# One cross-attention and FFN kernel: products, output pieces and value products in another order in the step list

## The chip, the cores and the metric

One core of a Trainium2 chip runs the whole layer. The time is device microseconds (us) of one execution, the median over runs; lower is better.

## The reference

Per batch row (8 of them, 128 tokens, width 512, 32 heads of 128), cut to what matters; everything is float32:

```python
h = rmsnorm(layernorm(x), ln_weight)                     # and hidden = layernorm(x)
h_q = (h @ w_q.T);  h_k = (ctx @ w_k.T);  h_v = (ctx @ w_v.T)
score = einsum('bqhd,bkhd->bhqk', h_q, h_k) + position_bias   # no scaling
score = where(mask, score, -inf);  p = where(mask, softmax(score), 0)
x = x + layernorm(x) + (p @ h_v) @ w_out.T
r = softmax(layernorm(x) @ gate_w.T)                     # 8 ways
x = x + (layernorm(x) * (r @ in_scale)) @ sign(weight).T * (r @ out_scale) + bias
```

## The kernel before

`schedule()` makes one list of steps. Every engine walks that same list and takes from it the steps it has a part in, so the place of a step sets its place in each engine's queue at once; semaphores do the rest. There is no other scheduler.

**Products.** Each float32 product is made of three TensorE passes (high by high, high by low, low by high), 128x512 each. The projections of a pair of heads go by a Strassen-like scheme: seven partial products `("P", n, i)` for a group n, each of six matmuls, in two PSUM banks. Products 1, 2, 7 and 4 go to the first bank of the pair (`proj0` from the groups after the first query pairs on), products 6, 5 and 3 to the second (`proj1`). Product 1 starts its bank anew, 2 adds to it, 7 starts it anew, 4 adds to it; 6 starts the second bank, 5 and 3 add to it. After each product its bank is read: 1 and 2 by ScalarE (L930, L934), 6 by VectorE at L1113, 5 at L1117, 7 at L1122, 3 at L1126 and 4 at L1131. A product waits until the reading of the one before it in its bank is done (`take`), as product 1 of a group does for L1131 of the group before. It also waits for its weights' low part, which GpSimd makes at L850 from what ScalarE rounds at L954 (steps `("WX", m, part)`).

**Attention units.** The main loop of `schedule()` runs p from 0 to 13. A pass makes four attention units (j = 4p to 4p + 3: two heads by two halves of the batch), the seven products of one query group, and the eight output pieces `("OUT", p - 1, b)` of the pair of heads before (six matmuls each). A unit j is: scores on TensorE (L1535), bias and mask added on VectorE (`SC`, L1270), row maximum (L1273), exponentials on ScalarE (L1008), normalising on VectorE (`N`: L1278, L1279, L1288), a turn of 32x32 blocks on VectorE (L1293), a way through DRAM that finishes the transpose, and the product with the values on TensorE (`PV`, L1561), two units later; then ScalarE rounds the result (`OH`, L1026) and VectorE makes the low part (`OL`, L1300). An output piece waits for `OL` and, in its PSUM bank (`out0` and `out1` in turn), for the addition (`ADD`, L1310 in the first pair, L1315 in the second, L1318 after them) of the piece two before it. GpSimd adds bias and mask (L862) and sums weights (L838 to L843).

**`aside(j, early, middle, late)`** writes one unit's stretch: `PV` of unit j - 2, scores and exponentials of unit j + 1, the early steps, the load of the turned probabilities, `N` and the turn of unit j + 1, then the middle and the late steps. Four calls make a pass. `outs(o, ...)` lists output pieces of the pair of heads before, `prod[i]` is product i with its reading, and `product(n - 1, 4)` the last product of the group before. The pass p = 0 is written out by hand, p = 1 has calls of its own, p = 2 to 13 share the rest, and p = 13 (`final`) has its own last call, since the last units (56 to 63) follow it in another manner.

## Time and profile before

| | |
|---|---|
| median of 3 runs | 805.37 us (805.34 to 806.15) |
| the profiled execution | 805.34 us, its span 803.5 us |
| granted TensorE clock | 1.000 of full speed over the span |
| TensorE busy | 796.5 us |
| VectorE, ScalarE, GpSimd busy | 637.7, 358.7, 306.6 us |

The span runs from the first to the last instruction; the other 1.84 us lie around it. An engine's busy time can be compared with the span directly. TensorE's records of successive matmuls overlap, since they are pipelined, so its step from start to start is what a matmul costs; 128x512 passes follow each other every 0.23 us.

### The profile page before, as it was taken

To read this page: it belongs to the slowest core of one execution; us is meant where nothing else is said; L and a number is where in the kernel's file an instruction comes from. 1 tells how busy PE (TensorE), PEld (TensorE's weight loads), DVE (VectorE), ACT (ScalarE), POOL (GpSimd) and SP (SyncE) were. 2 spreads that over 40 slices of the span, in tenths; PEclk is the share of its full clock that TensorE was granted. 3 is DMA by queue.
4 is the path that set the end of the run, shared out by engine and by line. 5 is a ranking of instruction groups with operands and counts; after the bars stand their busy time and mean duration, and the time that the engine had idled before them with its cause. 6 is when DMAs were issued, how large, how long until landed. Compare 5 with 4: busy or idle time off the path is not lost.

```text
span 803.5 us, 12698 instructions
## 1 busy us (share of the span) xinstructions
PE 796.5 (99%) x4090; PEld 673.5 (84%) x4090; DVE 637.7 (79%) x1066; ACT 358.7 (45%) x949; POOL 306.6 (38%) x279
## 2 busy tenths in 40 slices
PE   9999999999999999999999999999999999999998
PEld 7888888888888888887888888888888888888886
DVE  6877877886893696888888888888888887877675
ACT  6633432432341353644444444444454445446683
POOL 2113021020120033637445654644565464544136
PEclk9999999999999999999999999999999999999999
DMA  9455674584466558616755666575566557563002
GB/s 302 143 185 183 225 252 136 178 273 162 141 190 207 195 183 275 223 49 205 235 173 169 214 198 204 155 240 177 174 198 210 193 158 239 157 198 138 1 1 106
DMA packets 103217, 145.54 MB, mean 181 GB/s; under 512 B 9944, under 2 KB 74584, under 8 KB 97648
## 3 DMA queue, kind: packets, MB, share of 16 engines
q1 hardware_dynamic: 102720, 144.33, 55.3%
q8 instruction: 34, 0.56, 0.3%
q10 hardware_dynamic: 432, 0.39, 0.2%
q14 instruction: 31, 0.25, 0.1%
HBM read 93.31 MB, written 51.38 MB: 180 GB/s over the span
## 4 chain that ended last, share of the span: by engine, by line
PE 96%; DVE 2%; ACT 1%; issue 1%; DVEq 0%; ACTq 0%
PE out L1441 11%; PE out L1443 11%; PE out L1442 11%; PE proj L1441 10%; PE proj L1443 10%; PE proj L1442 10%; PE o L1561 7%; PE s L1535 7%; PE s L1443 4%; PE s L1441 4%; PE s L1442 4%; PE proj L1637 1%; PE proj L1638 1%; PE t L1589 1%; PE t L1545 1%
## 5 line engine op out<-in xcount | busy, mean ns | idle before, releaser
L1008 ACT ACTIVATE probs<-probs,neg_max 128x128 f32<-128x128 f32 x256 | 99.7, 391 | 124.5 <-DVE neg_max L1273 124.5
L838 POOL TENSOR_TENSOR w_stage<-w_stage 128x256 f32<-128x256 f32 x30 | 24.0, 800 | 264.7 <-DMA w_stage<-in_wk 238.6
L850 POOL TENSOR_TENSOR w_lo<-w_stage,w_hi 128x512 fp32r<-128x512 f32 (+1 forms) x52 | 64.2, 1245 | 133.8 <-ACT w_hi L954 133.8
L1441 PE MATMUL out<-wo_hi,o_hi 128*128 128x512 f32 x224 | 91.5, 409 | 0.0
L1443 PE MATMUL out<-wo_lo,o_hi 128*128 128x512 f32 x224 | 87.9, 392 | 0.0
L1441 PE MATMUL proj<-x_hi,w_hi 128*128 128x512 f32 x210 | 85.8, 409 | 1.8 <-DVE ring L1117 1.8
L1442 PE MATMUL out<-wo_hi,o_lo 128*128 128x512 f32 x224 | 87.4, 390 | 0.0
L862 POOL TENSOR_TENSOR bias_mask<-bias_raw,mask_neg 128x512 f32<-128x512 f32 x64 | 81.2, 1269 | 14.0 <-DVE probs L1270 13.8
L1443 PE MATMUL proj<-x_lo,w_hi 128*128 128x512 f32 x210 | 82.4, 392 | 0.0
L1442 PE MATMUL proj<-x_hi,w_lo 128*128 128x512 f32 x210 | 81.9, 390 | 0.0
L1318 DVE TENSOR_TENSOR acc<-out,acc 128x512 f32<-128x512 f32 x100 | 66.5, 675 | 8.2 <-PE out L1443 8.2
L954 ACT ACTIVATE w_hi<-w_stage 128x512 fp32r<-128x512 f32 (+1 forms) x113 | 61.7, 565 | 17.9 <-POOL w_stage L840 4.4
L1300 DVE TENSOR_TENSOR o_lo<-o,o_hi 128x512 fp32r<-128x512 f32 x60 | 41.2, 686 | 23.8 <-ACT o_hi L1026 23.8
L1026 ACT ACTIVATE o_hi<-o 128x512 fp32r<-128x512 f32 x60 | 35.4, 590 | 41.3 <-PE o L1561 41.2
L1441 PEld LDWEIGHTS out<-wo_hi,o_hi 128*128 128x128 f32 x224 | 42.2, 188 | 11.1 <-issue 3.7
L1138 DVE TENSOR_TENSOR w_lo<-w_stage,w_hi 128x512 fp32r<-128x512 f32 (+1 forms) x61 | 44.8, 735 | 7.3 <-ACT w_hi L954 6.6
L1443 PEld LDWEIGHTS out<-wo_lo,o_hi 128*128 128x128 f32 x224 | 42.0, 188 | 9.3
L1441 PEld LDWEIGHTS proj<-x_hi,w_hi 128*128 128x128 f32 x210 | 39.5, 188 | 11.2 <-DVE ring L1117 4.5
L1442 PEld LDWEIGHTS out<-wo_hi,o_lo 128*128 128x128 f32 x224 | 42.3, 189 | 7.4
L871 POOL TENSOR_TENSOR wo_lo<-wo_raw,wo_hi 128x1024 fp32r<-128x1024 f32 x14 | 34.0, 2428 | 37.4 <-ACT wo_hi L1034 37.4
L1008 ACT ACTIVATION_READ_ACCUMULATOR probs<-probs,neg_max 128x1 f32 x256 | 47.9, 187 | 0.0
L1443 PEld LDWEIGHTS proj<-x_lo,w_hi 128*128 128x128 f32 x210 | 39.4, 188 | 8.7
(360 smaller groups left out, 2080.1 us busy)
## 6 DMA issues: line engine op xcount, KB each, us to landing
k_spill<-ring SPq DMA_DIRECT2D x64, 256.0 KB, 3.5
v_spill<-ring SPq DMA_DIRECT2D x64, 256.0 KB, 2.5
p_turned<-probs SPq DMA_DIRECT2D x208, 64.0 KB, 1.8
probs_t<-p_turned SPq DMA_DIRECT2D x52, 256.0 KB, 4.0
big_stage<-in_wv SPq DMA_DIRECT2D x8, 1024.0 KB, 8.3
w_stage<-in_wq SPq DMA_DIRECT2D x32, 256.0 KB, 3.2
k_first<-k_spill SPq DMA_DIRECT2D x8, 1024.0 KB, 6.2
v_first<-v_spill SPq DMA_DIRECT2D x8, 1024.0 KB, 5.4
```

The costliest lines, as they stand in the source:

```text
L850: pool.tensor_tensor(lo, staged(m, part), hi.bitcast(F32), ALU.subtract).then_inc(g_wlo, 1)
L862: pool.tensor_tensor(bias_mask[:, j % 2], bias_raw[:, i % 2][:, None, :].to_broadcast([P, HALF, P]), mask_neg[:, halves[half], :], ALU.add ...
L954: act.activation(hi, staged(m, part), ACT.Copy).then_inc(a_whi, 1)
L1008: last = act.activation(probs[:, j % 2, b, :], probs[:, j % 2, b, :], ACT.Exp, bias=neg_max[:, col:col + 1], accum_out=row_sum[:, col:col ...
L1138: dve.tensor_tensor(lo, staged(m, part), hi.bitcast(F32), ALU.subtract).then_inc(v_wlo, 1)
L1300: dve.tensor_tensor(lo[:, h % 2], o_bank[:], hi[:, h % 2].bitcast(F32), ALU.subtract).then_inc(v_olo, 1)
L1318: dve.tensor_tensor(acc[:, b, :], bank_tensor[:], acc[:, b, :], ALU.add).then_inc(v_acc, 1)
L1441: pe.matmul(to[:], left_hi, right_hi, start=first and n == 0, stop=False, skip_group_check=True)
L1442: pe.matmul(to[:], left_lo, right_hi, start=False, stop=False, skip_group_check=True)
L1443: last = pe.matmul(to[:], left_hi, right_lo, start=False, stop=n == len(pairs) - 1, skip_group_check=True)
L1535: last = pe.matmul(to[:, b * P:(b + 1) * P], queries[:, b * P:(b + 1) * P], keys, start=True, stop=True)
L1561: last = pe.matmul(to[:, b * P:(b + 1) * P], v_tiles[p % 2][:, half * HALF + b, i * P:(i + 1) * P], moving, start=True, stop=True)
```

## The change

Only the order in the list changes; no instruction is added or taken away. In p = 0 the third output piece of the pair is taken in at the end. In p = 1 the pieces and products move among the four stretches: product 6 comes before the normalising of its stretch, product 2 to the end of it, product 5 a stretch earlier. In p = 2 to 13 the second output piece of the first stretch goes behind product 1. In p = 13 the value product of unit 54 goes behind product 3.

```diff
-                      *outs(0, 0), *normal(4), ("KL", 2), *sums, *outs(0, 1)]
+                      *outs(0, 0), *normal(4), ("KL", 2), *sums, *outs(0, 1, 2)]
...
         if p == 1:
-            steps += aside(j, outs(o, 2, 3) + prod[1], [("WX", m, 1)], [])
-            steps += aside(j + 1, load + outs(o, 4, 5), [*prod[6], ("VV", p + 1), ("WX", m, 2), ("WX", m, 3)], [])
-            steps += aside(j + 2, outs(o, 6) + prod[2], [*sums[:1], *outs(o, 7)], [("WO", p)])
-            steps += aside(j + 3, prod[5] + prod[7], [("WOL", p + 1), *prod[3], ("KL", p + 2), *sums[1:]], [])
+            steps += aside(j, outs(o, 3) + prod[1], [*outs(o, 4), ("WX", m, 1)], [])
+            steps += aside(j + 1, load + outs(o, 5) + prod[6], [("VV", p + 1), ("WX", m, 2), ("WX", m, 3)], prod[2])
+            steps += aside(j + 2, outs(o, 6), [*prod[5], *sums[:1], *outs(o, 7)], [("WO", p)])
+            steps += aside(j + 3, prod[7], [*prod[3], ("WOL", p + 1), ("KL", p + 2), *sums[1:]], [])
             continue
-        steps += aside(j, product(n - 1, 4) + outs(o, 0), [*outs(o, 1), *prod[1], ("WX", m, 1)], [])
+        steps += aside(j, product(n - 1, 4) + outs(o, 0), [*prod[1], ("WX", m, 1)], outs(o, 1))
...
         if final:
-            steps += aside(j + 3, prod[5] + prod[7], [("WOL", p + 1), ("PV", j + 2), *prod[3], *prod[4], ("KL", p + 2), ("WO", p + 1)],
+            steps += aside(j + 3, prod[5] + prod[7], [("WOL", p + 1), *prod[3], ("PV", j + 2), *prod[4], ("KL", p + 2), ("WO", p + 1)],
                            [*outs(p, 0, 1), ("PV", j + 3), ("VV", p + 2)])
```

TensorE in the first stretch of p = 2, from the last matmul of output piece (1, 0) in `out1` on. The rows give line, operation, result and inputs, and what a row waits for. Before, piece (1, 1) in `out0` follows and then product 1 in `proj0`:

```order
L1443 MATMUL out1<-wo_lo,o_hi 128x512
L1441 MATMUL out0<-wo_hi,o_hi 128x512 [waits v_acc,v_olo,g_wo_lo]
L1442 MATMUL out0<-wo_hi,o_lo 128x512
L1443 MATMUL out0<-wo_lo,o_hi 128x512
L1441 MATMUL out0<-wo_hi,o_hi 128x512
L1442 MATMUL out0<-wo_hi,o_lo 128x512
L1443 MATMUL out0<-wo_lo,o_hi 128x512
L1441 MATMUL proj0<-x_hi,w_hi 128x512 [waits g_wlo,v_read]
```

The same place with the change:

```order
L1443 MATMUL out1<-wo_lo,o_hi 128x512
L1441 MATMUL proj0<-x_hi,w_hi 128x512 [waits g_wlo,v_read]
L1442 MATMUL proj0<-x_hi,w_lo 128x512
L1443 MATMUL proj0<-x_lo,w_hi 128x512
L1441 MATMUL proj0<-x_hi,w_hi 128x512
L1442 MATMUL proj0<-x_hi,w_lo 128x512
L1443 MATMUL proj0<-x_lo,w_hi 128x512
L1441 MATMUL out0<-wo_hi,o_hi 128x512 [waits v_acc,v_olo,g_wo_lo]
```

Product 1 and its wait on VectorE's reading (`v_read`, L1131) stand six matmuls earlier. VectorE's own order is the same there.

VectorE in p = 1, from the addition of output piece (0, 6) on. Before:

```order
L1310 SCALAR_TENSOR_TENSOR acc<-acc,res_scale,out 128x512
L1278 RECIPROCAL inv_sum<-row_sum 128x4
L1279 TENSOR_TENSOR inv_sum<-inv_sum,row_valid 128x4
L1288 TENSOR_TENSOR t<-probs,inv_sum 128x512
L1293 STREAM_TRANSPOSE probs<-t 128x4x4x32
L1310 SCALAR_TENSOR_TENSOR acc<-acc,res_scale,out 128x512
L1300 TENSOR_TENSOR o_lo<-o,o_hi 128x512
L1270 TENSOR_TENSOR probs<-s,bias_mask 128x512
L1273 TENSOR_REDUCE neg_max<-probs 128x4
L1117 TENSOR_TENSOR ring<-proj,ring 128x512
L1122 TENSOR_TENSOR ring<-proj,ring 128x512
```

With the change:

```order
L1310 SCALAR_TENSOR_TENSOR acc<-acc,res_scale,out 128x512
L1278 RECIPROCAL inv_sum<-row_sum 128x4
L1279 TENSOR_TENSOR inv_sum<-inv_sum,row_valid 128x4
L1288 TENSOR_TENSOR t<-probs,inv_sum 128x512
L1293 STREAM_TRANSPOSE probs<-t 128x4x4x32
L1117 TENSOR_TENSOR ring<-proj,ring 128x512
L1310 SCALAR_TENSOR_TENSOR acc<-acc,res_scale,out 128x512
L1300 TENSOR_TENSOR o_lo<-o,o_hi 128x512
L1270 TENSOR_TENSOR probs<-s,bias_mask 128x512
L1273 TENSOR_REDUCE neg_max<-probs 128x4
L1122 TENSOR_TENSOR ring<-proj,ring 128x512
```

The reading of product 5 (L1117) stands ahead of the next unit's scores (L1270) instead of behind its maximum.

VectorE at the end of p = 13, as a difference:

```order
 L1279 TENSOR_TENSOR inv_sum<-inv_sum,row_valid 128x4
 L1288 TENSOR_TENSOR probs<-probs,inv_sum 128x512
-L1300 TENSOR_TENSOR o_lo<-o,o_hi 128x512
-L1126 TENSOR_TENSOR ring<-proj,ring 128x512
+L1126 TENSOR_TENSOR ring<-proj,ring 128x512
+L1300 TENSOR_TENSOR o_lo<-o,o_hi 128x512
 L1131 TENSOR_TENSOR ring<-proj,ring 128x512
 L1318 TENSOR_TENSOR acc<-out,acc 128x512 x2
```

The low part of unit 54's result (L1300) stands behind the reading of product 3.

## Rows read from the trace of the kernel before

**Rows 1.** The page's first part: busy us (share of the span) and instructions.

```profile
PE 796.5 (99%) x4090; PEld 673.5 (84%) x4090; DVE 637.7 (79%) x1066; ACT 358.7 (45%) x949; POOL 306.6 (38%) x279
```

**Rows 2.** Waits of TensorE, 330 to 700 us: waiting and releaser, us, times, longest.

```profile
PE proj L1441 <- DVE ring L1117: 1.8, 1, 1.8
```

**Rows 3.** Timeline of VectorE in p = 1: start, length, line, operation, idle before.

```profile
356.65 0.70 DVE L1310 SCALAR_TENSOR_TENSOR acc<-acc,res_scale,out 128x512 f32<-128x512 f32 x1
...
357.87 0.68 DVE L1270 TENSOR_TENSOR probs<-s,bias_mask 128x512 f32<-128x512 f32 x1
...
362.77 0.65 DVE L1270 TENSOR_TENSOR probs<-s,bias_mask 128x512 f32<-128x512 f32 x1
...
367.65 0.65 DVE L1113 TENSOR_TENSOR ring<-proj,ring 128x512 f32<-128x512 f32 x1
368.23 0.68 DVE L1300 TENSOR_TENSOR o_lo<-o,o_hi 128x512 fp32r<-128x512 f32 x1
368.82 0.68 DVE L1270 TENSOR_TENSOR probs<-s,bias_mask 128x512 f32<-128x512 f32 x1
...
372.75 1.19 DVE L1288 TENSOR_TENSOR t<-probs,inv_sum 128x512 f32<-128x512 f32 x1
...
375.84 0.68 DVE L1270 TENSOR_TENSOR probs<-s,bias_mask 128x512 f32<-128x512 f32 x1
...
377.15 0.68 DVE L1117 TENSOR_TENSOR ring<-proj,ring 128x512 f32<-128x512 f32 x1
```

**Rows 4.** Timeline of ScalarE in p = 1: two high parts of weights.

```profile
365.74 1.13 ACT L954 ACTIVATE w_hi<-w_stage 128x512 fp32r<-128x512 f32 x2
```

**Rows 5.** Timeline of TensorE around its only stall in the passes.

```profile
375.71 0.39 PE L1443 MATMUL proj<-x_lo,w_hi 128*128 128x512 f32 x1
377.88 0.50 PE L1441 MATMUL proj<-x_hi,w_hi 128*128 128x512 f32 x1 [1.79 <-DVE ring L1117]
378.22 0.39 PE L1442 MATMUL proj<-x_hi,w_lo 128*128 128x512 f32 x1
378.45 0.39 PE L1443 MATMUL proj<-x_lo,w_hi 128*128 128x512 f32 x1
```

**Rows 6.** Timeline of TensorE's weight loads at the same stall.

```profile
377.88 0.19 PEld L1441 LDWEIGHTS proj<-x_hi,w_hi 128*128 128x128 f32 x1 [2.21 <-DVE ring L1117]
```

**Rows 7.** Timeline of TensorE: output pieces' first matmuls, p = 2 and p = 13.

```profile
382.61 0.47 PE L1441 MATMUL out<-wo_hi,o_hi 128*128 128x512 f32 x1
...
384.07 0.40 PE L1441 MATMUL out<-wo_hi,o_hi 128*128 128x512 f32 x1
...
691.85 0.39 PE L1441 MATMUL out<-wo_hi,o_hi 128*128 128x512 f32 x1
```

**Rows 8.** Timeline of VectorE: p = 2, end of p = 2, first stretch of p = 13.

```profile
381.83 0.67 DVE L1300 TENSOR_TENSOR o_lo<-o,o_hi 128x512 fp32r<-128x512 f32 x1
...
383.74 0.68 DVE L1131 TENSOR_TENSOR ring<-proj,ring 128x512 f32<-128x512 f32 x1
...
407.37 1.22 DVE L1288 TENSOR_TENSOR t<-probs,inv_sum 128x512 f32<-128x512 f32 x1
...
691.54 0.68 DVE L1131 TENSOR_TENSOR ring<-proj,ring 128x512 f32<-128x512 f32 x1
```

**Rows 9.** Timeline of GpSimd at the end of p = 2.

```profile
407.31 0.72 POOL L850 TENSOR_TENSOR w_lo<-w_stage,w_hi 128x256 fp32r<-128x256 f32 x1 [0.99 <-ACT w_hi L954]
```

**Rows 10.** Line 1131, 370 to 740 us: ns min/median/max, first and last start.

```profile
L1131 DVE TENSOR_TENSOR ring<-proj,ring x13: 680/681/691, 383.7 to 717.5; 128x512 f32<-128x512 f32 x13
```

**Rows 11.** Timeline at the end of p = 13, TensorE: value product, first output piece.

```profile
713.70 1.05 PE L1561 MATMUL o<-probs_t,v_second 128*128 128x128 f32 x8
...
717.34 0.39 PE L1441 MATMUL out<-wo_hi,o_hi 128*128 128x512 f32 x1
```

**Rows 12.** The same place, ScalarE: high part of unit 54's result.

```profile
714.79 0.60 ACT L1026 ACTIVATE o_hi<-o 128x512 fp32r<-128x512 f32 x1
```

**Rows 13.** The same place, VectorE: low part of unit 54's result.

```profile
715.71 0.68 DVE L1300 TENSOR_TENSOR o_lo<-o,o_hi 128x512 fp32r<-128x512 f32 x1
```

## The prediction

> **What bounds the kernel now.** I read the busy times first: TensorE is busy for 796.5 of 803.5 us [rows 1], so some 7 us are all that any change of order can give, and most of that lies at the start and the end of the span. Then its waits in the passes of the main loop: there is one, 1.8 us, on the reading of product 5 (L1117) in p = 1 [rows 2]. Everywhere else TensorE goes through. So a change of order can win here once, and it can lose at every place where it puts a matmul ahead of what it needs. What is late at such a place is read from the timeline of VectorE beside that of TensorE.
>
> Two prices are needed throughout. **What a stall costs:** in p = 1 the matmul before it started at 375.71, so the next was due at 375.94 and the one after at 376.17, at 0.23 us a matmul (378.22 to 378.45 [rows 5]). L1117 ended at 377.15 + 0.68 = 377.83 [rows 3]; the matmul started at 377.88 and the second at 378.22 [rows 5]. So the second came 0.39 after the release, and the loss is 378.22 - 376.17 = 2.05 us, more than the 1.79 shown. As a rule: loss = release + 0.39 - (due + 0.23) = release + 0.16 - due. **What a product costs TensorE:** six matmuls, 1.37 us.
>
> **Part 1, p = 2 to 13: output piece 1 goes behind product 1.** VectorE's order doesn't change there, nor ScalarE's; only TensorE reaches product 1 six matmuls earlier. Product 1 starts bank `proj0` anew and so waits for L1131, which reads product 4 of the group before out of it. In p = 2 output piece 1 started at 384.07 [rows 7]; with the change product 1 is due then. L1131 ran from 383.74 to 384.42 [rows 8]: 0.35 too late, a loss of 0.51. In p = 13 it is 691.54 + 0.68 = 692.22 against 691.85 [rows 7, 8]: 0.37 late, a loss of 0.53. L1131 runs 13 times, the last in the final stretch [rows 10], so 12 passes have this pair, and the distance is between 0.35 and 0.37 in all of them. Nothing gives it back: L1131 can't come earlier, since VectorE goes without a break from the normalising of the stretch before (407.37 in p = 2 [rows 8]) to it, and the start of that is set by TensorE's product 7 in each pass anew, so all of it is shifted along with TensorE. What is behind the waiting matmul on TensorE, piece 1 and then the next unit's value product and scores, comes 0.5 later; VectorE's addition of piece 1 and all else wait for that or had slack. The earlier reading of product 1 by ScalarE frees ScalarE for L1026 a little sooner (some 0.1 us), which TensorE has no use for. Sum: 12 x 0.52 = **+6.2 us**. From below: if the restart costs only its 0.05 to the first matmul, 12 x 0.41 = 4.9.
>
> TensorE: Matmul & The Clock Gate in the Trainium skill (section Step-by-step: what each phase is for) says that weight loads are pulled ahead of running matmuls; by that rule the new stall would hide its load and cost 0.41 each, 4.9 in all. The trace doesn't show it for a matmul that waits: the load starts with the matmul, at 377.88, having waited for the same release [rows 6]. So 0.52 stands.
>
> **Part 2, p = 0 and 1: the stall at 376 goes, but what is late next?** VectorE and ScalarE run one chain here, unit by unit: scores plus bias (L1270), maximum, exponentials, normalising, turn, then whatever stands before the next L1270. The four L1270 start at 357.87, 362.77, 368.82 and 375.84 [rows 3], steps of 4.90, 6.05 and 7.02; and L1300 of unit 6, on which the first output piece of p = 2 waits, starts 5.99 after the last, at 381.83, ends at 382.50, and that piece starts at 382.61 [rows 7, 8]. So TensorE's start of p = 2 is set by this chain as much as the stall was. Operations between the maximum and the normalising lie beside the exponentials and are free; those between the turn and the next L1270 lengthen the chain. The change moves them so:
> - addition of piece 2 goes ahead of the first L1270, of piece 4 ahead of the second: +0.70 each [rows 3]. L1270s at 358.57 and 362.77 + 0.70 + 0.70 = 364.17.
> - the reading of product 6 (L1113) goes beside the exponentials: the step from 367.65 to 368.23, -0.58 [rows 3]. But L1300 of unit 4 behind it then waits for ScalarE: the two high parts start 2.97 after L1270 (365.74 - 362.77) [rows 3, 4], so at 367.14, and take 1.13; then come product 2's reading and L1026, 0.60 each [rows 12]; a length runs some 0.1 into the next one's start. That is 369.27 for L1300, and L1270 follows 0.59 later (368.23 to 368.82) at 369.86: 1.04 later than before.
> - product 5's reading (L1117) goes from beside the exponentials into the chain: +0.60. L1288 at 372.75 took 1.19 because GpSimd was at its weight sums; how the two meet now is the open term. Without any meeting the stretch loses up to 0.9, with the same one nothing; I take 0.3 less than before.
> So the last L1270 comes at 369.86 + 7.02 + 0.60 - 0.3 = 377.2, and L1300 of unit 6 ends at 377.2 + 5.99 + 0.67 = 383.9. The first output piece of p = 2 starts 0.11 after that, at 384.0, instead of 382.61. TensorE doesn't stall at product 3 any more (L1117 ends at about 376), reaches that piece at 380.6 and waits there for some 3.3 us. The stall is moved, and it grows: **+1.4 us** (0.75 to 1.7 by the meeting of L1288 with GpSimd). A lesser point: product 6 now wants its weights at 364.05 and GpSimd has them at about 364.0; up to 0.2 is lost there, but inside the 3.3.
>
> SBUF — State Buffer in the Trainium skill (section Who interferes with whom) has an exclusive lock for VectorE's operations with two SBUF inputs against GpSimd; the rows agree, L1288 took 1.22 while L850 held 0.72 of it [rows 8, 9].
>
> **Part 3, the end of p = 13: value product of unit 54 behind product 3.** The value product started at 713.70 [rows 11] and L1026 1.09 later, at 714.79 [rows 12]; L1300 waited for nothing but VectorE at 715.71 [rows 13]. Behind product 3 the value product starts at 715.07, L1026 at 716.16, L1300 at 716.79, and ends at 717.47. The first output piece, which needs it, is due at 717.34 as before [rows 11]: loss 717.47 + 0.16 - 717.34 = **+0.3 us**.
>
> **The sum** against the profiled execution, 805.34 us (0.03 under the median, so the same): 805.34 + 6.2 + 1.4 + 0.3 = **813.2 us**. Its own range: 0.75 + 4.9 + 0 below, 811.0; above 1.7 + 6.4 + 0.5 and a little for terms unseen, 814.5. SyncE's and GpSimd's orders don't change, and the turned probabilities have two units' time to come back, so no DMA comes into it.
>
> **The rivals.**
> - The stall at 376 falls away and nothing takes its place: 805.34 - 2.05 = 803.3, faster. It needs L1131 at least 0.5 earlier against TensorE in 12 passes, and L1300 of unit 6 at least 2 earlier. For it: the stall is real. Against it: both operations stand where they stood on VectorE.
> - The chain in p = 1 isn't as stiff as I read it and the stall does vanish, while the wait on L1131 costs its 6.2 and the end 0.3: 805.34 - 2.05 + 6.5 = 809.8. For it: p = 1 is a sum of many terms. Against it: two operations more in the chain.
> - The wait on L1131 resolves itself: L1288 ran 1.22 instead of 0.70 since GpSimd began 0.06 before it [rows 8, 9]. If the new order parts the two, L1131 comes 0.52 earlier and product 1 loses nothing: 805.34 + 1.7 = 807.0. Against it: both follow ScalarE's exponentials in that stretch, whose order is the same.
> - The earlier reading of product 1 moves GpSimd's L850 in the first stretch and the later piece 1 moves VectorE's additions; if L1288 of the second stretch now meets GpSimd (before they missed each other by about 0.1 us) and the 0.5 reaches TensorE, 12 x 0.52 more: 819.4. Against it: VectorE waits for ScalarE again before the next L1300, which takes that up.
> - The moves have no effect that can be told from none, the gain in p = 1 paying for shorter waits elsewhere.
>
> **How the numbers follow.** The forecast has 0.68, the second rival 0.10, the third 0.07, the fourth 0.07, the first 0.06, no effect 0.02. Predicted is 813.2. To hold 8 in 10 the range takes in the second rival and the forecast's own: 809.5 to 815.0. A measurement of this kernel tells about 0.2% (1.6 us) from no change; the third rival is at the edge of that and counts as slower. Faster 0.06, the same 0.03, slower 0.91.
>
> **What would show it.** After the change the waits of TensorE must have product 1 (L1441 in `proj`) behind L1131, 12 times, 0.2 to 0.4 us each by the profile's count; the first output piece of p = 2 must wait about 3 us, with L1300 as releaser or just ahead; the wait on L1117 must be gone or under 0.6. The pass lasted (691.85 - 384.07) / 11 = 27.98 us before [rows 7] and must last 28.5. If TensorE shows no wait on L1131, part 1 is wrong and with it the sign's size; if the first piece of p = 2 starts before 382.6, part 2 is wrong.

## The result, and the profile after

| | before | after |
|---|---|---|
| median | 805.76 us (805.34 to 806.17) | 814.55 us (813.24 to 814.86) |
| the profiled execution | 805.34 us, span 803.5 | 813.57 us, span 811.8 |
| granted TensorE clock over the span | 1.000 | 1.000 |
| TensorE busy | 796.5 us | 800.1 us |

The change makes the kernel slower by 8.8 us: after over before is 1.0106, 95% interval 1.0089 to 1.0124. Forecast were 813.2 us and a range of 809.5 to 815.0. The profiled execution took 8.2 us more.

The page of the changed kernel, busy us of each engine; it answers to [rows 1]:

```profile
PE 800.1 (99%) x4090; PEld 672.0 (83%) x4090; DVE 637.4 (79%) x1066; ACT 360.3 (44%) x949; POOL 306.8 (38%) x279
```

The 8 us don't stand out there: a matmul that waited has a longer record (0.50 instead of 0.39), and short gaps go unseen. The waits of the changed kernel's TensorE in the same stretch as [rows 2], 330 to 705 us (us, times, longest), show them at once:

```profile
PE proj L1441 <- DVE ring L1131: 3.1, 12, 0.3
PE out L1441 <- issue: 2.4, 1, 2.4
PE o L1561 <- DMA probs_t<-p_turned: 0.4, 1, 0.4
```

The wait on L1117 is gone. In its place stand the twelve waits of product 1, one long wait of an output piece, and a short one of a value product that wasn't foreseen. First the repeated one: VectorE's reading of product 4 at the start of p = 2 of the changed kernel, then TensorE from the last matmul of output piece 0 on, and the first output piece of p = 13:

```profile
385.08 0.68 DVE L1131 TENSOR_TENSOR ring<-proj,ring 128x512 f32<-128x512 f32 x1
```

```profile
385.18 0.39 PE L1443 MATMUL out<-wo_lo,o_hi 128*128 128x512 f32 x1
385.82 0.50 PE L1441 MATMUL proj<-x_hi,w_hi 128*128 128x512 f32 x1 [0.25 <-DVE ring L1131]
386.15 0.39 PE L1442 MATMUL proj<-x_hi,w_lo 128*128 128x512 f32 x1
...
697.74 0.47 PE L1441 MATMUL out<-wo_hi,o_hi 128*128 128x512 f32 x1
```

Product 1 was due at 385.18 + 0.23 = 385.41 and its second matmul at 385.64; that came at 386.15. The loss is 0.51, of which the profile counts 0.25 as idle. L1131 ended at 385.76, so release + 0.16 - due gives 385.76 + 0.16 - 385.41 = 0.51 as well. The first output piece of p = 2 starts at 383.95 (below), that of p = 13 at 697.74: a pass lasts (697.74 - 383.95) / 11 = 28.53 us, and was 27.98 [rows 7].

Now p = 1. VectorE of the changed kernel, to be laid beside [rows 3] and [rows 8]:

```profile
356.10 0.72 DVE L1293 STREAM_TRANSPOSE probs<-t 128x512 f32<-128x512 f32 x1
...
358.63 0.68 DVE L1270 TENSOR_TENSOR probs<-s,bias_mask 128x512 f32<-128x512 f32 x1
...
364.15 0.68 DVE L1270 TENSOR_TENSOR probs<-s,bias_mask 128x512 f32<-128x512 f32 x1
...
369.88 0.68 DVE L1270 TENSOR_TENSOR probs<-s,bias_mask 128x512 f32<-128x512 f32 x1
...
373.21 0.22 DVE L1279 TENSOR_TENSOR inv_sum<-inv_sum,row_valid 128x4 f32<-128x4 f32 x1
373.47 1.19 DVE L1288 TENSOR_TENSOR t<-probs,inv_sum 128x512 f32<-128x512 f32 x1
...
375.33 0.65 DVE L1117 TENSOR_TENSOR ring<-proj,ring 128x512 f32<-128x512 f32 x1
...
377.15 0.68 DVE L1270 TENSOR_TENSOR probs<-s,bias_mask 128x512 f32<-128x512 f32 x1
...
383.17 0.67 DVE L1300 TENSOR_TENSOR o_lo<-o,o_hi 128x512 fp32r<-128x512 f32 x1
```

Two more rows of VectorE from the kernel before, to compare with 356.10 and 373.21:

```profile
356.01 0.72 DVE L1293 STREAM_TRANSPOSE probs<-t 128x512 f32<-128x512 f32 x1
...
372.15 0.56 DVE L1279 TENSOR_TENSOR inv_sum<-inv_sum,row_valid 128x4 f32<-128x4 f32 x1
```

And TensorE of the changed kernel, where the stall of before was ([rows 5]) and where the new one is:

```profile
376.21 0.40 PE L1441 MATMUL proj<-x_hi,w_hi 128*128 128x512 f32 x1
...
378.10 1.16 PE L1561 MATMUL o<-probs_t,v_second 128*128 128x128 f32 x8 [0.36 <-DMA probs_t<-p_turned]
...
381.15 0.40 PE L1443 MATMUL proj<-x_lo,w_hi 128*128 128x512 f32 x1
383.95 0.47 PE L1441 MATMUL out<-wo_hi,o_hi 128*128 128x512 f32 x1 [2.40 <-issue]
```

Product 3 goes through at 376.21 without a wait. The output piece was due at 381.38 and waits until 383.95. The profile names "issue", which is no releaser; L1300 of unit 6 had ended at 383.84, 0.11 before, and is the one: of what else this piece waits for, VectorE's last L1310 had ended at 376.64 and GpSimd's last L871 at 377.63. So the stall moved from product 3 to the first output piece of p = 2, and grew.

### The profile page after: what moved, and what is told of

Its sections match the earlier page's. It is cut to its first block, busy times and chain, and to the rows that moved or that the text cites. A ratio compares the mean times of both kernels' runs of the same rounds, so it can differ in the third digit from the quotient of the medians.

```text
span 811.8 us, 12698 instructions
## 1 busy us (share of the span) xinstructions
PE 800.1 (99%) x4090; PEld 672.0 (83%) x4090; DVE 637.4 (79%) x1066; ACT 360.3 (44%) x949; POOL 306.8 (38%) x279
## 4 chain that ended last, share of the span: by engine, by line
PE 81%; DVE 10%; issue 4%; ACT 4%; DMA 0%; ACTq 0%; DVEq 0%
PE out L1441 10%; PE out L1443 10%; PE out L1442 10%; PE proj L1441 8%; PE proj L1443 8%; PE proj L1442 8%; PE o L1561 4%; PE s L1535 4%; PE s L1442 4%; PE s L1443 4%; PE s L1441 4%; ACT probs L1008 2%; DVE probs L1270 2%; DVE t L1288 2%; DVE neg_max L1273 1%
## 5 line engine op out<-in xcount | busy, mean ns | idle before, releaser
L850 POOL TENSOR_TENSOR w_lo<-w_stage,w_hi 128x512 fp32r<-128x512 f32 (+1 forms) x52 | 63.9, 1238 | 140.5 <-ACT w_hi L954 140.5
L1300 DVE TENSOR_TENSOR o_lo<-o,o_hi 128x512 fp32r<-128x512 f32 x60 | 41.2, 687 | 28.0 <-ACT o_hi L1026 27.8
L871 POOL TENSOR_TENSOR wo_lo<-wo_raw,wo_hi 128x1024 fp32r<-128x1024 f32 x14 | 33.6, 2401 | 38.7 <-ACT wo_hi L1034 38.7
```

The costliest lines, as they stand in the source:

```text
L850: pool.tensor_tensor(lo, staged(m, part), hi.bitcast(F32), ALU.subtract).then_inc(g_wlo, 1)
L871: pool.tensor_tensor(lo, wo_raw[:], hi.bitcast(F32), ALU.subtract).then_inc(g_wo_lo, 1)
L1300: dve.tensor_tensor(lo[:, h % 2], o_bank[:], hi[:, h % 2].bitcast(F32), ALU.subtract).then_inc(v_olo, 1)
```

## The experiments

Each kernel is the kernel before with the edit shown. Times of one batch are compared with runs of the kernel before on the same chip: 805.73 us for the first four, 805.78 for the next four, 805.65 for the last four. In edits, `("ONLY", ...)` writes a part of a step alone, where the plain step would bring its companion with it (an output piece its addition, `PV` its `OH` and `OL`).

### The three parts, one by one

**Part 1 alone**, p = 2 to 13:

```diff
-        steps += aside(j, product(n - 1, 4) + outs(o, 0), [*outs(o, 1), *prod[1], ("WX", m, 1)], [])
+        steps += aside(j, product(n - 1, 4) + outs(o, 0), [*prod[1], ("WX", m, 1)], outs(o, 1))
```

> Only the move in p = 2 to 13: output piece 1 behind product 1. Theory (a matmul put ahead of the reading it needs): product 1 waits for L1131 in each of 12 passes, 0.2 to 0.4 us each as the profile counts idle time, 0.52 us each in real loss with the restart; 805.7 + 6.2 = 811.9 us (810.6 if a stall costs only what the profile shows as idle and 0.05 for the restart). The stall on L1117 in p = 1 stays, 1.8. Rival (the moves of p = 0 and 1 carry the loss): within 1 us of before.

Measured: 812.02 us (811.62 to 812.38), ratio 1.0078, interval 1.0066 to 1.0090, so +6.3. Waits of its TensorE:

```profile
PE proj L1441 <- DVE ring L1131: 3.1, 12, 0.3
PE proj L1441 <- DVE ring L1117: 1.6, 1, 1.6
```

Twelve waits, 3.1 us by the profile, cost 6.3 us of time. The rule with 0.52 a stall holds, the counted idle of 0.26 doesn't. The old stall on L1117 is still there, so nothing is given back elsewhere.

**Part 2 alone**, p = 0 and 1:

```diff
-                      *outs(0, 0), *normal(4), ("KL", 2), *sums, *outs(0, 1)]
+                      *outs(0, 0), *normal(4), ("KL", 2), *sums, *outs(0, 1, 2)]
...
-            steps += aside(j, outs(o, 2, 3) + prod[1], [("WX", m, 1)], [])
-            steps += aside(j + 1, load + outs(o, 4, 5), [*prod[6], ("VV", p + 1), ("WX", m, 2), ("WX", m, 3)], [])
-            steps += aside(j + 2, outs(o, 6) + prod[2], [*sums[:1], *outs(o, 7)], [("WO", p)])
-            steps += aside(j + 3, prod[5] + prod[7], [("WOL", p + 1), *prod[3], ("KL", p + 2), *sums[1:]], [])
+            steps += aside(j, outs(o, 3) + prod[1], [*outs(o, 4), ("WX", m, 1)], [])
+            steps += aside(j + 1, load + outs(o, 5) + prod[6], [("VV", p + 1), ("WX", m, 2), ("WX", m, 3)], prod[2])
+            steps += aside(j + 2, outs(o, 6), [*prod[5], *sums[:1], *outs(o, 7)], [("WO", p)])
+            steps += aside(j + 3, prod[7], [*prod[3], ("WOL", p + 1), ("KL", p + 2), *sums[1:]], [])
```

> Only the moves in p = 0 and 1. Theory (the chain of VectorE and ScalarE from unit to unit is what ends there, two operations longer): the wait on L1117 is gone, the first output piece of p = 2 waits some 2.4 us for L1300, as in the changed kernel; 805.7 + 1.4 = 807.1 us. Rival (the stall on L1117 was the bound): 2 us faster than before, 803.7.

Measured: 807.68 us (806.75 to 809.52), ratio 1.0025, interval 1.0015 to 1.0035. The eight executions fall into two groups: 806.75 to 807.03 with a granted clock of 1.000 over the span, and 808.34 to 809.52 with 0.995 to 0.997. The first group is +1.2 and agrees with the chain as worked out. The second has something more, and the profiled execution (809.52) is one of it. Its windows of 2 us (after the window: busy us of the engines; the third number from the end is PEclk, the granted clock):

```profile
380.00:382.00 2.00, 1.14 (x5) 0.57 (x4) 1.43 (x3) 1.25 (x5) 1.15 (x2) 1.00 0.65 166
382.00:384.00 2.00, 0.00 (x0) 0.00 (x0) 1.97 (x5) 0.00 (x0) 1.13 (x1) 0.87 0.11 29
384.00:386.00 2.00, 1.84 (x5) 1.50 (x5) 1.94 (x4) 0.59 (x3) 0.00 (x0) 0.50 0.47 111
...
390.00:392.00 2.00, 2.00 (x13) 1.73 (x12) 0.41 (x1) 0.58 (x2) 0.00 (x0) 0.92 0.93 333
```

Its TensorE there:

```profile
377.80 1.05 PE L1561 MATMUL o<-probs_t,v_second 128*128 128x128 f32 x8
...
384.16 0.77 PE L1441 MATMUL out<-wo_hi,o_hi 128*128 128x512 f32 x1 [3.02 <-issue]
384.72 0.63 PE L1442 MATMUL out<-wo_hi,o_lo 128*128 128x512 f32 x1
...
390.26 0.43 PE L1443 MATMUL proj<-x_lo,w_hi 128*128 128x512 f32 x1
```

During the wait of 3.02 us the clock goes from 1.00 to 0.50, that is from 2.4 to 1.2 GHz, and stays there for some 6 us of work. From 384.72 to 390.26 there are 13 steps of 0.43 instead of 0.23, which is 13 x 0.20 = 2.6 us, and the step before them took 0.56 instead of 0.31: 2.9 us in all, where 809.52 lies 2.6 over the group at 806.9. The prediction has no term for it.

**Part 3 alone**, the value product of unit 54:

```diff
-            steps += aside(j + 3, prod[5] + prod[7], [("WOL", p + 1), ("PV", j + 2), *prod[3], *prod[4], ("KL", p + 2), ("WO", p + 1)],
+            steps += aside(j + 3, prod[5] + prod[7], [("WOL", p + 1), *prod[3], ("PV", j + 2), *prod[4], ("KL", p + 2), ("WO", p + 1)],
```

> Only the move in p = 13: the value product of unit 54 behind product 3. Theory: the output piece behind product 4 waits for L1300, a loss of 0.3 us, 806.0 us, which a time can hardly tell from before; the profile can, by the start of that piece against the value product before it. Rival: no loss at all.

Measured: 806.16 us (805.13 to 809.33), ratio 1.0007, interval 0.9998 to 1.0015. By time alone it can't be told from nothing. The timeline of this kernel shows the loss, first TensorE, then VectorE's L1300:

```profile
717.86 0.39 PE L1443 MATMUL proj<-x_lo,w_hi 128*128 128x512 f32 x1
718.34 0.47 PE L1441 MATMUL out<-wo_hi,o_hi 128*128 128x512 f32 x1
718.65 0.39 PE L1442 MATMUL out<-wo_hi,o_lo 128*128 128x512 f32 x1
```

```profile
717.55 0.69 DVE L1300 TENSOR_TENSOR o_lo<-o,o_hi 128x512 fp32r<-128x512 f32 x1 [0.44 <-ACT o_hi L1026]
```

The second matmul was due at 717.86 + 0.46 = 718.32 and came at 718.65: 0.33, where 0.3 was worked out; in the changed kernel the same three matmuls start at 725.08, 725.54 and 725.85, which is 0.31. The profile counts no wait of a matmul here: by the records TensorE stands still from 718.25 to 718.34 only.

### Is it the reading, or the order of TensorE?

Product 1 waits for L1131 because VectorE does the next unit's scores and maximum first. This kernel has TensorE's order of part 1, and VectorE reads product 4 (L1131, the step `C21`) ahead of the scores (L1270, `SC`):

```diff
-        steps += aside(j, product(n - 1, 4) + outs(o, 0), [*outs(o, 1), *prod[1], ("WX", m, 1)], [])
+        first = aside(j, product(n - 1, 4) + outs(o, 0), [*prod[1], ("WX", m, 1)], outs(o, 1))
+        first[first.index(("S", j + 1))] = ("ONLY", ("S", j + 1))
+        first.insert(first.index(("C21", n - 1)) + 1, ("ONLY", ("SC", j + 1)))
+        steps += first
```

> The move in p = 2 to 13 as in the run of that move alone, TensorE's order the same to the matmul, but on VectorE the reading of product 4 (L1131) stands ahead of the next unit's scores (L1270), not behind its maximum. Theory (product 1 waits for L1131 and for nothing else): L1131 ends at about 0.7 after product 4, some 0.6 before product 1 is due; the 12 waits are gone, and the scores, some 0.9 later, are taken up by VectorE's idle time before L1300 in the next three stretches: 805.7 us within 0.5. Rival (TensorE's own order, its bank changes, costs the time): 811.9 as with the move alone. Third: the later scores reach product 3 or the next pass's first output piece and cost part of it, 807 to 810.

Measured: 805.97 us (805.32 to 806.42), ratio 1.0001, interval 0.9993 to 1.0010. The wait on L1131 is gone from the list. VectorE and TensorE of this kernel in p = 3:

```profile
411.51 0.69 DVE L1131 TENSOR_TENSOR ring<-proj,ring 128x512 f32<-128x512 f32 x1 [0.23 <-PE proj L1443]
412.12 0.68 DVE L1270 TENSOR_TENSOR probs<-s,bias_mask 128x512 f32<-128x512 f32 x1
```

```profile
411.38 0.47 PE L1441 MATMUL out<-wo_hi,o_hi 128*128 128x512 f32 x1
...
412.84 0.39 PE L1441 MATMUL proj<-x_hi,w_hi 128*128 128x512 f32 x1
```

Now L1131 waits for the product and not the product for L1131; product 1 starts 1.46 after the piece, six matmuls as they run elsewhere, with nothing lost. All of part 1's 6.2 us hang on where that one reading of 0.68 us stands; what TensorE's order costs by itself is too small to be told from nothing, 0.8 us at most by the interval.

### Small losses that the profile doesn't count

If a stall costs release + 0.16 - due, it also costs something where the release comes a little before the matmul is due. In p = 3 of the kernel before, for one, L1300 ends at 410.51 and the first output piece is due at 410.56, 0.05 later. This kernel moves the reading of product 3 (L1126, `C12`), which stands ahead of L1300, behind the next unit's maximum:

```diff
-            steps += aside(j + 3, prod[5] + prod[7], [("WOL", p + 1), *prod[3], ("KL", p + 2), *sums[1:]], [])
+            steps += aside(j + 3, prod[5] + prod[7], [("WOL", p + 1), prod[3][0], ("KL", p + 2), *sums[1:]], [])
...
-        steps += aside(j, product(n - 1, 4) + outs(o, 0), [*outs(o, 1), *prod[1], ("WX", m, 1)], [])
+        steps += aside(j, [("C12", n - 1)] + product(n - 1, 4) + outs(o, 0), [*outs(o, 1), *prod[1], ("WX", m, 1)], [])
...
         else:
-            steps += aside(j + 3, prod[5] + prod[7], [("WOL", p + 1), *prod[3], ("KL", p + 2), *sums[1:]], [])
+            steps += aside(j + 3, prod[5] + prod[7], [("WOL", p + 1), prod[3][0], ("KL", p + 2), *sums[1:]], [])
```

> The kernel before, with one move on VectorE alone: the reading of product 3 (L1126) stands behind the next unit's maximum in p = 2 to 13 instead of ahead of L1300. The first output piece of each pass waits for L1300 now (0.11 from its end to the piece, the weights' load late by 0.29), a loss of 0.13 a pass by the rule release + 0.16 - due. Theory (that rule holds for waits too short to be counted as TensorE's idle time): L1300 0.58 earlier, 12 x 0.13 = 1.5 us faster, 804.2. Rival (only idle time that the profile counts is lost time): no change, 805.7.

Measured: 803.54 us (802.92 to 804.56), ratio 0.9974, interval 0.9963 to 0.9986: 2.2 us faster than the kernel before. The weight loads' waits of the whole span, before and then in this kernel:

```profile
PEld out L1441 <- issue: 4.5, 15, 0.3
```

```profile
PEld out L1441 <- issue: 0.8, 3, 0.3
```

Twelve short waits of 0.3 are gone, and they were waits of weight loads, not of matmuls. Product 4 to product 1 of p = 3 took 409.09 to 413.45 = 4.36 us before and 409.00 to 413.19 = 4.19 here; 12 x 0.17 = 2.0 of the 2.2. Of the 0.17, 0.13 lies at the piece itself, as expected; the cause of the rest wasn't looked for. The rule for a late release holds here too: 410.51 + 0.16 - 410.56 = 0.11.

### How stiff is the chain in p = 1?

**L1113 and the addition of piece (0, 7) beside the exponentials**, which should shorten the chain by two operations:

```diff
-            steps += aside(j + 1, load + outs(o, 4, 5), [*prod[6], ("VV", p + 1), ("WX", m, 2), ("WX", m, 3)], [])
-            steps += aside(j + 2, outs(o, 6) + prod[2], [*sums[:1], *outs(o, 7)], [("WO", p)])
-            steps += aside(j + 3, prod[5] + prod[7], [("WOL", p + 1), *prod[3], ("KL", p + 2), *sums[1:]], [])
+            steps += aside(j + 1, load + outs(o, 4, 5) + prod[6], [("VV", p + 1), ("WX", m, 2), ("WX", m, 3)], [])
+            steps += aside(j + 2, outs(o, 6) + prod[2], [*sums[:1], ("ONLY", ("OUT", o, 7))], [("WO", p)])
+            steps += aside(j + 3, prod[5] + [("ONLY", ("ADD", o, 7))] + prod[7], [("WOL", p + 1), *prod[3], ("KL", p + 2), *sums[1:]], [])
```

> The kernel before, TensorE's order the same, VectorE's changed in p = 1 alone: the reading of product 6 (L1113) and the addition of output piece 7 stand beside the exponentials instead of ahead of the scores. Theory (chain): 1.21 out of the chain, some 0.38 back because three operations don't fit beside one set of exponentials; the reading of product 5 (L1117) is 0.9 to 1.0 earlier, the stall of 1.8 shrinks to 0.9, and 804.8 us. Rival (what GpSimd's lock does to L1288 decides, and eats it): 805.7.

Measured: 806.36 us (805.64 to 808.83), ratio 1.0015, interval 1.0004 to 1.0026. A miss: no gain. The seven executions at a clock of 1.000 have a median of 805.95, so most of the 0.6 is the clock. TensorE waits 2.3 us for L1117, where it waited 1.8 [rows 2]. VectorE, and GpSimd beside it:

```profile
366.80 1.27 DVE L1279 TENSOR_TENSOR inv_sum<-inv_sum,row_valid 128x4 f32<-128x4 f32 x1
368.10 1.75 DVE L1288 TENSOR_TENSOR t<-probs,inv_sum 128x512 f32<-128x512 f32 x1
```

```profile
366.77 2.53 POOL L850 TENSOR_TENSOR w_lo<-w_stage,w_hi 128x512 fp32r<-128x512 f32 x2 [1.97 <-ACT w_hi L954]
```

L1279 takes 0.16 where nothing is beside it; here it began 0.03 after GpSimd's first of two 1.26 us operations and ended with it, and L1288 (0.70 alone) then lost to the second. That is 1.11 + 1.05 = 2.16 us on the chain. In return the next stretch, where the kernel before loses 0.40 + 0.49 = 0.89 by L1279 (0.56) and L1288 (1.19), loses nothing here: they take 0.16 and 0.70. The lock's net cost is 1.27, which eats the 1.2 that was taken out, and from the first to the last L1270 it is 18.53 us where it was 17.97 [rows 3]. SBUF — State Buffer in the Trainium skill (section Who interferes with whom) calls the ports that VectorE and GpSimd share an exclusive lock, and says that the order of issue decides who is blocked; these rows agree, twice in a row.

**Both of the last two edits together**; the last call of p = 1 then reads:

```diff
-            steps += aside(j + 3, prod[5] + prod[7], [("WOL", p + 1), *prod[3], ("KL", p + 2), *sums[1:]], [])
+            steps += aside(j + 3, prod[5] + [("ONLY", ("ADD", o, 7))] + prod[7], [("WOL", p + 1), prod[3][0], ("KL", p + 2), *sums[1:]], [])
```

> Both of the two last moves together. Theory: they add up, 0.9 and 1.5, 803.3 us, with TensorE stalled once in the passes, for 0.9 us. Rival: the one takes from the other, 804 or more.

Measured: 805.69 us (803.36 to 806.77), ratio 0.9994, interval 0.9985 to 1.0003. A miss. L1279 and L1288 took 0.96 and 1.76, the wait at product 3 was 2.0, and seven of eleven executions had a granted clock of 0.997 or 0.998 and took 805.4 to 806.8; the four at 0.999 or above took 803.4 to 804.8. So most of the gain of the moved reading is there at the higher clock, and the stall in p = 1 takes it back where the clock falls.

**Part 2 with the additions of pieces 2 and 4 beside the exponentials**, to see whether the +0.70 each is what part 2 pays:

```diff
-                      *outs(0, 0), *normal(4), ("KL", 2), *sums, *outs(0, 1, 2)]
+                      *outs(0, 0), *normal(4), ("KL", 2), *sums, *outs(0, 1), ("ONLY", ("OUT", 0, 2))]
...
-            steps += aside(j, outs(o, 3) + prod[1], [*outs(o, 4), ("WX", m, 1)], [])
-            steps += aside(j + 1, load + outs(o, 5) + prod[6], [("VV", p + 1), ("WX", m, 2), ("WX", m, 3)], prod[2])
+            steps += aside(j, [("ONLY", ("ADD", o, 2))] + outs(o, 3) + prod[1], [("ONLY", ("OUT", o, 4)), ("WX", m, 1)], [])
+            steps += aside(j + 1, load + [("ONLY", ("ADD", o, 4))] + outs(o, 5) + prod[6], [("VV", p + 1), ("WX", m, 2), ("WX", m, 3)], prod[2])
```

> The moves of p = 0 and 1 as in the run of those alone, TensorE's order the same to the matmul, but VectorE's additions of output pieces 2 and 4 stand behind the next maximum, beside the exponentials, instead of ahead of the next scores. Theory (the end of p = 1 is set by the chain of VectorE and ScalarE, which the move made two operations longer): the chain loses 1.40 less 0.25 for the third operation beside the second exponentials, so L1300 of unit 6 ends 1.1 to 1.4 earlier, the first output piece of p = 2 waits 1.2 us instead of 2.4 to 3.0, the clock stays at its upper level, and the time is that of before within 0.5: 805.8 us. Rival (TensorE's order in p = 1 costs the time): 807 or more, as with the move.

Measured: 808.44 us (808.16 to 809.46), ratio 1.0038, interval 1.0026 to 1.0051. A miss, and for the same reason as the one above: the chain is shorter at its start and not at its end. The two rows of VectorE where the gain goes, and the wait that stays:

```profile
368.75 0.69 DVE L1300 TENSOR_TENSOR o_lo<-o,o_hi 128x512 fp32r<-128x512 f32 x1 [0.43 <-ACT o_hi L1026]
...
372.70 0.62 DVE L1279 TENSOR_TENSOR inv_sum<-inv_sum,row_valid 128x4 f32<-128x4 f32 x1
```

```profile
383.82 0.47 PE L1441 MATMUL out<-wo_hi,o_hi 128*128 128x512 f32 x1 [2.94 <-issue]
```

VectorE comes early and waits for ScalarE (0.43, and 0.26 once before), and then L1279 meets GpSimd's weight sums (0.62, where part 2 alone has 0.21). From the turn ahead of the moved addition to the first output piece of p = 2 it is 383.82 - 356.13 = 27.69 us, and 384.16 - 356.33 = 27.83 in part 2 alone: 0.14 of the expected 1.1 to 1.4. This chain can't be read as a plain sum of its operations' lengths. All five executions had a clock of 0.995 to 0.998, so their 808.44 is to be laid beside the 808.8 of part 2's executions at the lower clock, and not beside 806.9.

**Only the addition of piece (0, 7)** beside the exponentials, L1113 where it was:

```diff
-            steps += aside(j + 2, outs(o, 6) + prod[2], [*sums[:1], *outs(o, 7)], [("WO", p)])
-            steps += aside(j + 3, prod[5] + prod[7], [("WOL", p + 1), *prod[3], ("KL", p + 2), *sums[1:]], [])
+            steps += aside(j + 2, outs(o, 6) + prod[2], [*sums[:1], ("ONLY", ("OUT", o, 7))], [("WO", p)])
+            steps += aside(j + 3, prod[5] + [("ONLY", ("ADD", o, 7))] + prod[7], [("WOL", p + 1), *prod[3], ("KL", p + 2), *sums[1:]], [])
```

> The kernel before with one operation moved: in p = 1 VectorE does the addition of output piece (0, 7) (L1310) behind the reading of product 5 (L1117), beside the exponentials, instead of between the turn and the next L1270. Theory of the stiff chain: the last L1270 of p = 1 comes 0.63 earlier less about 0.1 for GpSimd's lock, at some 375.3 instead of 375.84, L1117 ends at 377.3, the stall of TensorE at product 3 shrinks from 1.8 to about 1.3, and the kernel takes 0.5 to 0.6 us less: 805.2. Rival (the lock, as when L1113 was moved too): with VectorE's L1288 starting in another moment against GpSimd's weight sums, L1279 and L1288 take longer by as much as was won: stall of 1.8 or more, 805.8 or above. Here the L1288 that runs against GpSimd in the stretch before isn't moved, so I hold the first for likelier, 2 to 1.

Measured: 804.91 us (804.42 to 805.85), ratio 0.9987, interval 0.9979 to 0.9996: 0.7 us faster. Its TensorE:

```profile
376.86 0.50 PE L1441 MATMUL proj<-x_hi,w_hi 128*128 128x512 f32 x1 [0.70 <-DVE ring L1117]
```

The profiled execution shows more than the edit takes out: the last L1270 comes 17.03 after the first, against 17.97 [rows 3], 0.63 for the addition and the rest because L1279 took 0.28 in it and 0.56 before. Whether the lock's share changes from one execution of this kernel to the next, which span 1.4 us, isn't shown; the kernel with both gains, below, has the same order up to there, and in its trace L1279 took 0.56 again.

**Part 2 with the reading of product 5 (L1117) back beside the exponentials**, against part 2:

```diff
-            steps += aside(j + 2, outs(o, 6), [*prod[5], *sums[:1], *outs(o, 7)], [("WO", p)])
-            steps += aside(j + 3, prod[7], [*prod[3], ("WOL", p + 1), ("KL", p + 2), *sums[1:]], [])
+            steps += aside(j + 2, outs(o, 6), [prod[5][0], *sums[:1], *outs(o, 7)], [("WO", p)])
+            steps += aside(j + 3, [prod[5][1]] + prod[7], [*prod[3], ("WOL", p + 1), ("KL", p + 2), *sums[1:]], [])
```

> Part 2 of the change alone, with the reading of product 5 (L1117) put back to where it was, beside the exponentials of the next unit. It settles the third item of part 2 of the prediction (L1117 in the chain costs 0.60). Theory: the last L1270 of p = 1 comes 0.6 earlier than with part 2 alone (at some 376.5 instead of 377.1), TensorE stalls at product 3 again, by about 2.4, and the first output piece of p = 2 starts 0.6 earlier than with part 2 alone, at some 383.3, having waited little: 806.9 - 0.6 = 806.3 for executions with the clock at 1.00. Rival: the meeting with GpSimd changes again and the 0.60 isn't had back: 806.9 or more. In either case the stall of 2.4 may bring the clock down to 0.50 for some us in part of the executions, which adds 1.5 to 2.5 to those.

Measured: 806.36 us (805.78 to 807.68), ratio 1.0011, interval 1.0002 to 1.0019. The eight executions at a clock of 1.000 took 805.78 to 806.51, the four at 0.998 took 806.93 to 807.68. The last L1270 and the reading:

```profile
376.85 0.68 DVE L1270 TENSOR_TENSOR probs<-s,bias_mask 128x512 f32<-128x512 f32 x1
...
378.16 0.68 DVE L1117 TENSOR_TENSOR ring<-proj,ring 128x512 f32<-128x512 f32 x1
```

```profile
378.90 0.50 PE L1441 MATMUL proj<-x_hi,w_hi 128*128 128x512 f32 x1 [2.25 <-DVE ring L1117]
...
383.63 0.47 PE L1441 MATMUL out<-wo_hi,o_hi 128*128 128x512 f32 x1
```

From the first L1270 (358.91) to the last it is 17.94, in part 2 alone 358.85 to 377.38 = 18.53: 0.59 for L1117, as worked out, and the executions at a clock of 1.000 are 0.7 us faster than those of part 2 alone (806.2 against 806.9). And in this kernel TensorE stands for 2.25 at product 3 and reaches the first output piece with almost nothing to wait for: one and the same delay shows at either place. That is what "the stall is moved" means.

### A version that beats both

**The reading of product 3 late, and the addition of piece (0, 7) beside the exponentials**, the two edits that gained; both diffs stand above, and the last call of p = 1 is that of the kernel with both of the two edits.

> The kernel before with two edits: the addition of piece (0, 7) beside the exponentials in p = 1, and in p = 2 to 13 the reading of product 3 (L1126) behind the next unit's maximum. The second alone gave 803.54. Theory that the two add: 803.54 - 0.6 = 802.9, and TensorE's one stall at product 3 of p = 1 at about 1.3. Rival: the addition of piece (0, 7) gives nothing, or its later place in front of the reading of product 3 costs what it gives: 803.5.

Measured: 803.27 us (802.66 to 803.51), ratio 0.9966, interval 0.9954 to 0.9978. TensorE waits 1.1 on L1117, more than the 0.7 with the addition alone, for the most part since L1279 took 0.56 and not 0.28. The 0.3 below 803.54 is less than the 0.6 expected and within the spread of both.

**The same, with TensorE's value product of unit 6 ahead of product 3**, to fill the stall:

```diff
-        found = [("PV", j - 2)] if j - 2 in BLOCKED else [("PV", 3)] if j == 4 else []
+        found = [("ONLY", ("OH", 6), ("OL", 6))] if j == 8 else [("PV", j - 2)] if j - 2 in BLOCKED else [("PV", 3)] if j == 4 else []
...
-            steps += aside(j + 3, prod[5] + [("ONLY", ("ADD", o, 7))] + prod[7], [("WOL", p + 1), prod[3][0], ("KL", p + 2), *sums[1:]], [])
+            steps += aside(j + 3, prod[5] + [("ONLY", ("ADD", o, 7))] + prod[7], [("WOL", p + 1), ("ONLY", ("PV", 6)), prod[3][0], ("KL", p + 2), *sums[1:]], [])
```

> The two edits of the run before and a third: in p = 1 TensorE does the value product of unit 6 (L1561, 0.89 us of TensorE) ahead of product 3 instead of behind it, so that it runs while product 3 waits for the reading of product 5 (L1117). VectorE's order is that of the run before. Theory that the stall is only an order of TensorE: the value product's operands are there at about 375.5, it starts at about 376 when TensorE would idle, the stall at product 3 shrinks from 1.3 to about 0.4, and the kernel takes 0.9 us less than without it: 802.0. The idle being short, the granted clock should stay at 1.00 there in all executions. Rival: what ends the stretch is the chain of VectorE up to L1300 of unit 6, before which the first output piece of p = 2 waits; then the gain at product 3 turns into a wait of that piece, and the time stays at 802.9. Second rival: the value product waits for the DMA that brings the turned probabilities, by 0.4 as in the changed kernel; 802.4.

Measured: 802.89 us (802.29 to 803.48), ratio 0.9963, interval 0.9952 to 0.9975: the fastest, 2.8 us under the kernel before, though not to be told from the one above it (803.27). Its only wait in the passes:

```profile
PE o L1561 <- DMA probs_t<-p_turned: 0.9, 1, 0.9
```

The wait on L1117 is gone, and the value product waits in its place, for the turned probabilities to come back. That is the second rival of the expectation, with a wait of 0.9 where it had 0.4; so little of the 1.1 is won, and the time is the 802.9 that the first rival had, but not for its reason: the first output piece of p = 2 doesn't wait here.

## Why the prediction came right

**Part 1, 6.2 us: right, with its mechanism.** Part 1 alone measured +6.3, with twelve waits of product 1 on L1131. The price of a stall was the step that mattered: 4.9 if the load were hidden, 3.1 by the profile's own count, 6.2 by the rule. The weight load is held up with its matmul; the changed kernel's loads show 0.7 for each where its matmuls show 0.3:

```profile
PEld proj L1441 <- DVE ring L1131: 8.2, 12, 0.7
```

The third rival, L1131 coming earlier, would have shown as no wait. The fourth, a second collision, would have made the pass 28.53 + 0.52 = 29.05 us; it lasts 28.53, and L1288 of the second stretch, at 387.29, still takes 0.70. The reading moved by hand took all of it away, which is the other side of the same proof. One reading of the prediction was a little off: of L1288's 1.22 us GpSimd's L850 overlaps 0.66 and not 0.72, as it had begun 0.06 earlier; no sum uses it.

**Part 2, 1.4 us: right in its mechanism, and a little too large in its size at full clock.** The chain was forecast operation by operation:

| | forecast | changed kernel |
|---|---|---|
| L1270, first | 358.57 | 358.63 |
| second | 364.17 | 364.15 |
| third | 369.86 | 369.88 |
| last | 377.2 | 377.15 |
| first output piece of p = 2 | 384.0 | 383.95 |

That the times of the table agree to hundredths is luck in part. In ten of the kernels here, which have the same order up to the first L1270, it starts anywhere from 357.79 to 358.68, so distances are the better test. From the turn (L1293) ahead of it to the first output piece of p = 2 it was 382.61 - 356.01 = 26.60 us; it is 27.85 in the changed kernel and 27.83 with part 2 alone: +1.25 and +1.23, where +1.4 was forecast. The two additions were put at +0.70 each, their length, and cost 0.67 and 0.62, as a length runs into the next one's start. The last term took 0.3 off for a meeting of L1288 with GpSimd, a choice between 0 and 0.9 without a row behind it. Its size came true by another operation: L1288 took 1.19 as before, and L1279 in front of it 0.22 instead of 0.56. It was 0.21 and 0.23 in the two other kernels of this order, so it isn't the luck of one execution; but where the order differs, the lock took between 0.6 and 2.2 us from the first to the last L1270, and the prediction couldn't know which.

The wait at the output piece was put at 3.3 and counted at 2.4 in the changed kernel, and at 3.0 in part 2 alone. The difference is that TensorE reached the piece at 381.38 and not at 380.6, in part for a reason the prediction had ruled out ("no DMA comes into it"): the value product of unit 6 was due at 377.58 and started at 378.10, as its turned probabilities weren't back. In part 2 alone it started at 377.80, without a wait; so the DMA is late in some executions and not in all. Those 0.5 us cost nothing, as they lie ahead of the longer wait. The direction of part 2 is shown (+1.2 at full clock); that it could be had to a tenth isn't.

**Part 3, 0.3 us: 0.31 in the timeline of the changed kernel and 0.33 by itself**, and too small to be measured as a time.

**The sum.** 813.2 was forecast; the profiled execution took 813.57, the median is 814.55. The parts measured one by one, 6.3 + 1.2 (at full clock) + 0.3, on 805.76 give 813.6, so they add up and don't act on each other much. What the sum left out is the clock. Of the five executions of the changed kernel two had 0.998 over the span, and took 814.68 and 814.86; those at 1.000 took 813.24, 813.57 and 814.43. So the clock explains a part of the 1.3 us between forecast and median, and the spread of the rest isn't explained. The stated range held it, with 0.45 us to spare above; the sum's own upper end, 814.5, is just below it.

**The rivals.** That the stall vanishes and nothing takes its place fell with the wait of 2.4 us. The second, a chain that isn't stiff, fell in the changed kernel but is half true: with L1113 moved (two kernels) and with the additions of pieces 2 and 4 moved, ScalarE and the lock took all or nearly all of it back, while the addition of piece (0, 7) alone kept its 0.63 and L1117 put back its 0.59. That nothing can be told from no change fell with the interval, 1.0089 to 1.0124.

## What to carry to other kernels

Before a product is moved earlier on the engine that sets the time, look up when its buffer's last reading ends on the other engine; a reading 0.35 us late costs 0.51 us each time, in every pass, and may be cured by moving that one reading. Look also for waits of weight loads of 0.2 to 0.3 us that repeat once a pass: they don't appear as waits of matmuls, and twelve of them were worth 2.2 us here. (Eleven more, of 0.2 us, stand at product 3 of the kernel before, behind L1117. In p = 2 the step there is 405.94 to 406.24, 0.30 instead of 0.23, so they may be worth 11 x 0.07 = 0.8 us by this estimate; no run tried it.) A chain over several engines isn't a sum of lengths; when one of its operations shares a lock with another engine, every move re-deals who comes first.

## What the runs showed of the hardware

**A wait of 2 to 3 us of TensorE can halve its clock, in one execution and not in the next.** The changed kernel's windows over its wait of 2.4 us, in its profiled execution, against those of part 2 alone above:

```profile
382.00:384.00 2.00, 0.05 (x1) 0.09 (x1) 2.00 (x4) 0.00 (x0) 0.92 (x1) 1.00 0.15 37
384.00:386.00 2.00, 1.75 (x7) 1.15 (x8) 1.97 (x4) 0.80 (x5) 0.00 (x0) 1.00 0.44 105
```

Here the clock stays at 1.00. Over all timed executions the mean granted clock was 0.998 or less in:

| kernel | longest wait in p = 1, us | executions at 0.998 or less |
|---|---|---|
| addition of piece (0, 7) beside | 0.7 | 0 of 12 |
| the two fastest | 0.9 and 1.1 | 0 of 11 |
| part 1 alone; reading 4 first; reading 3 late | 1.6 to 1.8 | 0 of 23 |
| before, in the three batches; part 3 alone | 1.8 and 1.7 | 7 of 84 |
| L1113 and addition beside, with and without reading 3 late | 2.0 and 2.3 | 11 of 22 |
| part 2, reading of product 5 beside | 2.3 | 4 of 12 |
| the changed kernel | 2.4 | 2 of 5 |
| part 2 alone | 3.0 | 4 of 8 |
| part 2, additions beside | 2.9 | 5 of 5 |

In the kernels with waits of 2.0 to 3.0 us of which both kinds were seen (the changed one apart) the executions with the lower clock took 1.3 to 2.1 us longer (part 2 alone: 808.8 against 806.9, each the middle of its group). The correspondence isn't perfect: one execution of the kernel with L1113 moved took 808.82 at 1.000. Only in a profile can the place of the fall be seen: with both edits (L1113 and the addition, reading 3 late) work resumed at 378.63, and the steps were still 0.23 up to 379.89, 1.26 us later, before they grew. For the executions without a profile it is inferred from their mean clock, and not shown, that the fall belongs to this wait. What decides whether a wait of this length lowers the clock wasn't found; the number of executions is too small for a rule. So a stall of TensorE has a second price that its own length doesn't show, and a kernel with two groups of times is to be read by its granted clock before a theory is made of them. TensorE: Matmul & The Clock Gate in the Trainium skill (section What's actually happening) has the clock at one of two levels by how busy TensorE has been; the windows agree, 1.00 and 0.50.

**Small shifts settle who has the lock, and it can be lost twice.** L1279, an operation of 0.16 us on 128x4 elements, took 1.27 when it began 0.03 after GpSimd, and L1288 behind it 1.75 instead of 0.70 since GpSimd went straight on to its next. In the two kernels with L1113 moved this falls on the second stretch of p = 1 and the third is free of it; in all others the second is free and in the third they take 0.21 to 0.62 and 1.19 to 1.20.
